# Attention over sources: five groups in different stages per round, and TensorE's order written anew

## What is computed

```python
feat   = concatenate([x[src], edge_weights, x[dst]], axis=1)     # 64 + 16 + 64
h      = relu(feat @ W_att1.T + b_att1)                          # 144 wide
scores = (h @ W_att2.T + b_att2)[:, 0]
m      = segment_max(scores, src)
e      = exp(scores - m[src])
denom  = segment_sum(e, src)
msg    = segment_sum(e / denom[src] * lin_x[dst], src)
```

## Time and profile before

| | us |
|---|---|
| median of 3 runs | 23699.2 (23693.9 to 23703.35) |
| the profiled execution | 23729.27 |
| its span | 23727.5 |
| `source_attention` in it: first gather to last sum | 14451.5 to 19048.4 |
| POOL's 3520 gathers in it (L1724) | 3350.7 busy |
| TensorE's granted clock over the span | 0.625 of full |

### The profile page before, as it was taken

How to read it: one execution, slowest core, us unless ns; L and a number is a source line. 1 busy time by engine, 2 the same in 40 slices (tenths; PEclk the granted TensorE clock), 3 DMA queues, 4 the chain that set the end, 5 groups by cost and what they waited for, 6 DMA issues and landing times. The chain is left out here.

```text
span 23727.5 us, 309845 instructions
## 1 busy us (share of the span) xinstructions
PE 8267.3 (35%) x52022; PEld 6762.3 (29%) x52023; DVE 10675.2 (45%) x28947; ACT 6494.6 (27%) x15429; POOL 16160.3 (68%) x16650
## 2 busy tenths in 40 slices
PE   2431111111111111111111116888888753333334
PEld 1110000000000111111111115777787733333333
DVE  4744444444444322222222216777777554444445
ACT  0012222222222133333333323555555411111111
POOL 1057777777777477777777774777777527777773
PEclk7755555555555555555555557999999755555555
DMA  9223333333333122222222225777777823333333
GB/s 413 82 61 78 81 80 79 79 81 79 78 81 80 43 73 72 71 72 72 71 72 72 71 58 61 86 86 86 86 86 86 66 37 60 60 60 60 60 60 34
DMA packets 2547246, 1881.33 MB, mean 79 GB/s; under 512 B 1939077, under 2 KB 2190275, under 8 KB 2525087
## 3 DMA queue, kind: packets, MB, share of 16 engines
q1 hardware_dynamic: 1766148, 1106.93, 21.6%
q0 software_dynamic: 536736, 602.92, 15.8%
q10 hardware_dynamic: 244252, 170.38, 2.5%
HBM read 1244.80 MB, written 635.40 MB: 79 GB/s over the span
## 5 line engine op out<-in xcount | busy, mean ns | idle before, releaser
L1724 POOL DMA_INDIRECT H<-tab,a_rs x3520 | 3350.7, 952 | 1434.6 <-issue 970.7
L1994 POOL DMA_INDIRECT g_G<-tab,g_rs x3232 | 3065.4, 948 | 1364.6 <-issue 1000.9
L912 POOL DMA_INDIRECT PT<-tab,m_idx x3125 | 3209.2, 1027 | 955.1 <-issue 952.4
L891 POOL DMA_INDIRECT rec<-PT,posi x3125 | 3064.9, 981 | 952.9 <-issue 952.6
L912 POOL DMA_INDIRECT PT<-tab,t_idx x3125 | 2976.5, 952 | 957.8 <-issue 952.1
L1107 PE MATMUL t_ps_z<-t_w,t_eaT 128*128 128x512 f32 x1000 | 671.2, 826 | 5563.9 <-DVE ACC L1081 2789.4
L2075 PE MATMUL g_ps_a<-g_zr,g_oh 128*128 128x64 f32 x6464 | 1586.5, 427 | 2578.9 <-ACT g_zr L2056 2144.2
L2075 PEld LDWEIGHTS g_ps_a<-g_zr,g_oh 128*128 128x128 f32 x6464 | 1438.7, 327 | 2726.7 <-issue 1996.5
L1107 PEld LDWEIGHTS t_ps_z<-t_w,t_eaT 128*128 128x128 f32 x1000 | 265.7, 291 | 5987.9 <-issue 5984.8
L1042 DVE TENSOR_TENSOR t_ps_z<-t_ps_z,PT 128x1600 f32<-128x1600 f32 x125 | 229.1, 1833 | 3256.9 <-DMA PT<-tab,t_idx 3256.9
L2024 DVE TENSOR_TENSOR ACC<-ACC,g_ps_a 128x64 f32 x3232 | 715.5, 221 | 1925.7 <-DVE ACC L2024 1550.0
(11 more groups left out here) (423 smaller groups left out, 23574.2 us busy)
## 6 DMA issues: line engine op xcount, KB each, us to landing
PT<-expand SPq DMA_DIRECT2D x250, 800.0 KB, 4.5
rec<-H SPq DMA_DIRECT2D x88, 1640.0 KB
a_rs<-rec SPq DMA_DIRECT2D x880, 164.0 KB
a_row<-keyc SPq DMA_DIRECT2D x880, 128.0 KB
sums<-t_So SPq DMA_DIRECT2D x125, 850.0 KB
expand<-H ACTq DMA_DIRECT2D x80, 1250.0 KB
PT<-in_ea SPq DMA_DIRECT2D x625, 160.0 KB
maxima<-m_So SPq DMA_DIRECT2D x125, 800.0 KB
```

The lines of the kernel that those rows point to most:

```text
L891: pool.indirect_dma_start(rec, bass.IndirectOffsetOnAxis(ap=self.posi[:, q, t:t + 1], axis=0), rbi[:, q, t, :], None).then_inc(self.s_sc[q ...
L912: pool.indirect_dma_start(G[:, q, c, :], None, table, bass.IndirectOffsetOnAxis(ap=idx[:, q, c:c + 1], axis=0)).then_inc(s_g[q], 16)
L1724: pool.indirect_dma_start(G[:, k, t, 0:D], None, tab3, bass.IndirectOffsetOnAxis(ap=rs[:, k, t, 1:2], axis=0)).then_inc(s_g[k], 16)
L1994: pool.indirect_dma_start(G[:, k, t, :], None, tab3, bass.IndirectOffsetOnAxis(ap=rs[:, k, t, 1:2], axis=0)).then_inc(s_g[k], 16)
```

## The change

Every stage of a group moves to its own round, so that DVE and PE each work on five groups in one round:
- DVE: scores(g), maxima(g-1), exponents(g-2), keep(g-4), onehots(g+2), weighted(g-2).
- PE: node_sums(g-3), feature_rows(g+1), key_rows(g+1), turn(g+2), spread(g), edge_maxima(g-1).
- ACT: high_part(g), rescale(g-1), weights(g-2), penalty(g), turned(g+2), local_keys(g+5), features(g+5).

`ps_z`, `ss`, `hi`, `mn`, `dd` and `p` get two slots and `lg` four; `ps_a` has one slot where it had two. The table `M` goes: the old maximum is the last group's maximum times `same` plus `less`, two tables made once from `blk` (1 and 0 where the next group is of the same block, else 0 and -LOW), so ACT reads no block number; DVE reads one in `keep`, right ahead of its use, in every round. PE gets four more `settle`. SP's and POOL's programs stay, but for a count of 3 in POOL's first wait. POOL's wait for `node_sums` of group g - 8 stays too, and `node_sums` of a group now stands in round g+3 where it stood in g+1, while its `turn` stands in g-2 where it stood in g-3.

```diff
-                G, oh = in_place_of_h(ctx, ("a_G", U, GW), ("a_oh", SLOTS, P))
+                taken = T * (U * GW + SLOTS * P)
+                assert taken + NG <= NB * D
+                G = hw[:, 0:T * U * GW].rearrange("p (k t c) -> p k t c", k=U, t=T)
+                oh = hw[:, T * U * GW:taken].rearrange("p (k t c) -> p k t c", k=SLOTS, t=T)
+                same = hw[:, taken:taken + NG]
+                less = sbl("less", [P, NG])
...
-                ps_z = ps_in(ctx, "a_ps_z", [P, 2, 512])
+                ps_z = ps_in(ctx, "a_ps_z", [P, 2, 2, 512])
                 ps_lb = ps_in(ctx, "a_ps_lb", [P, GE])
                 ps_m = ps_in(ctx, "a_ps_m", [P, 512])
-                ps_a = ps_in(ctx, "a_ps_a", [P, 2, 512])
-                zv = [ps_z[:, b, 0:tpb * width].rearrange("p (t c) -> p t c", t=tpb) for b in range(2)]
+                ps_a = ps_in(ctx, "a_ps_a", [P, 512])
...
+                        dve.memset(same[:, 0:1], 0.0).then_inc(s_set, 1)
+                        dve.tensor_tensor(same[:, 1:NG], blk[:, 1:NG], blk[:, 0:NG - 1], ALU.is_equal).then_inc(s_same, 1)
+                        dve.wait_ge(s_set, 3)
+                        dve.wait_ge(s_same, 1)
+                        dve.tensor_scalar(less[:], same, LOW, -LOW, ALU.mult, ALU.add).then_inc(s_same, 1)
...
-                        def maxima(g, k, r, b):
+                        def maxima(g, k, r):
+                            q = k % 2
                             dve.wait_ge(s_lb, g + 1)
                             dve.wait_ge(s_pen, g + 1)
                             dve.wait_ge(s_mo, g + 1)
-                            at_least(dve, s_mb, g)
-                            at_least(dve, s_me, g)
+                            at_least(dve, s_me, g - 1)
+                            at_least(dve, s_corr, g - 1)
+                            at_least(dve, s_mn, g)
                             settle(dve)
-                            dve.tensor_tensor_reduce(junk[:], ps_lb[:], pen[:, k % 2], 1.0, mo[:, k % 2:k % 2 + 1], ALU.add, ALU.max, mn[:]).then_inc(s_mn, 1)
+                            dve.tensor_tensor_reduce(junk[:], ps_lb[:], pen[:, q], 1.0, mo[:, q:q + 1], ALU.add, ALU.max, mn[:, q:q + 1]).then_inc(s_mn, 1)
...
-                        def keep(g, k, r, b):
+                            dve.tensor_scalar(dd[:, q], dd[:, q], 70.0, None, ALU.min).then_inc(s_d, 1)
+
+                        def keep(g, k, r):
+                            b = dve.value_load(blk[0:1, bass.ds(g, 1)], min_val=0, max_val=NB)
                             acc = ACC[:, bass.ds(b, 1), 0:VC].rearrange("p a c -> p (a c)")
                             dve.wait_ge(s_corr, g + 1)
                             dve.wait_ge(s_acc, g + 1)
                             at_least(dve, s_done, g)
                             settle(dve)
-                            dve.scalar_tensor_tensor(acc, acc, corr[:, k % SLOTS:k % SLOTS + 1], ps_a[:, k % 2, 0:VC], ALU.mult, ALU.add).then_inc(s_done, 1)
-
-                        blocks = [None] * U
-
-                        def body(g, k, r):
-                            at = (g, k, r)
+                            dve.scalar_tensor_tensor(acc, acc, corr[:, k % SLOTS:k % SLOTS + 1], ps_a[:, 0:VC], ALU.mult, ALU.add).then_inc(s_done, 1)
+
+                        def body(*at):
                             stage(scores, 0, NG, *at, unroll=U)
-                            stage(weighted, 1, NG, *at, unroll=U)
+                            stage(maxima, 1, NG, *at, unroll=U)
+                            stage(exponents, 2, NG, *at, unroll=U)
+                            stage(keep, 4, NG, *at, unroll=U)
                             stage(onehots, -2, NG, *at, unroll=U)
-                            older = None
-                            if not isinstance(g, int) or g >= 2:
-                                older = blocks[k - 2] if k >= 2 else block_of(g - 2)
-                            if not isinstance(g, int) or g < NG:
-                                blocks[k] = block_of(g)
-                                maxima(g, k, r, blocks[k])
-                            if older is not None:
-                                keep(g - 2, (k - 2) % U, r + (k - 2) // U, older)
-                            stage(exponents, 0, NG, *at, unroll=U)
+                            stage(weighted, 2, NG, *at, unroll=U)
                         onehots(0, 0, 0)
                         onehots(1, 1, 0)
-                        pipeline(dve, NG, body, 2, unroll=U)
+                        pipeline(dve, NG, body, 4, unroll=U)
...
                         def node_sums(g, k, r):
                             pe.wait_ge(s_oh, g + 1)
-                            at_least(pe, s_done, g - 1)
+                            at_least(pe, s_done, g)
+                            settle(pe)
                             for t in range(T):
-                                mm = pe.matmul(ps_a[:, k % 2, 0:VC], oh[:, k % SLOTS, t, :], G[:, k, t, 0:VC],
+                                mm = pe.matmul(ps_a[:, 0:VC], oh[:, k % SLOTS, t, :], G[:, k, t, 0:VC],
                                                start=(t == 0), stop=(t == T - 1))
                             mm.then_inc(s_acc, 1)
 
                         def body(*at):
+                            stage(node_sums, 3, NG, *at, unroll=U)
                             stage(feature_rows, -1, NG, *at, unroll=U)
+                            stage(key_rows, -1, NG, *at, unroll=U)
+                            stage(turn, -2, NG, *at, unroll=U)
                             stage(spread, 0, NG, *at, unroll=U)
-                            stage(key_rows, -1, NG, *at, unroll=U)
-                            stage(edge_maxima, 0, NG, *at, unroll=U)
-                            stage(node_sums, 1, NG, *at, unroll=U)
-                            stage(turn, -3, NG, *at, unroll=U)
+                            stage(edge_maxima, 1, NG, *at, unroll=U)
                         turn(0, 0, 0)
+                        turn(1, 1, 0)
                         feature_rows(0, 0, 0)
                         key_rows(0, 0, 0)
-                        turn(1, 1, 0)
-                        turn(2, 2, 0)
-                        pipeline(pe, NG, body, 1, unroll=U)
+                        pipeline(pe, NG, body, 3, unroll=U)
...
-                            act.activation(corr[:, k % SLOTS:k % SLOTS + 1], mn[:], ACT.Exp, bias=mo[:, k % 2:k % 2 + 1], scale=-1.0).then_inc(s_corr, 1)
-                            act.copy(M[:, bass.ds(block_of(g), 1)], mn[:]).then_inc(s_mb, 1)
+                            act.activation(corr[:, k % SLOTS:k % SLOTS + 1], mn[:, q:q + 1], ACT.Exp, bias=mo[:, q:q + 1], scale=-1.0).then_inc(s_corr, 1)
                             if not is_group(g, NG - 1):
-                                act.wait_ge(s_mb, g + 1)
-                                old_maximum(*after(g, k, r, U))
-
-                        def block_of(g):
-                            return act.value_load(blk[0:1, bass.ds(g, 1)], min_val=0, max_val=NB)
-
-                        def old_maximum(g, k, r):
-                            at_least(act, s_corr, g - 1)
-                            act.copy(mo[:, k % 2:k % 2 + 1], M[:, bass.ds(block_of(g), 1)]).then_inc(s_mo, 1)
...
                             stage(high_part, 0, NG, *at, unroll=U)
+                            stage(rescale, 1, NG, *at, unroll=U)
+                            stage(weights, 2, NG, *at, unroll=U)
+                            stage(penalty, 0, NG, *at, unroll=U)
                             stage(turned, -2, NG, *at, unroll=U)
                             stage(local_keys, -5, NG, *at, unroll=U)
                             stage(features, -5, NG, *at, unroll=U)
-                            stage(penalty, -1, NG, *at, unroll=U)
-                            stage(rescale, 0, NG, *at, unroll=U)
-                            stage(weights, 0, NG, *at, unroll=U)
-                        act.wait_ge(s_set, 2)
-                        old_maximum(0, 0, 0)
+                        act.wait_ge(s_set, 3)
+                        act.wait_ge(s_same, 2)
+                        act.copy(mo[:, 0:1], mo[:, 0:1]).then_inc(s_mo, 1)
                         for g in range(5):
                             local_keys(g, g, 0)
-                            if g < 4:
-                                features(g, g, 0)
+                            features(g, g, 0)
                         for g in range(2):
                             turned(g, g, 0)
-                        penalty(0, 0, 0)
-                        features(4, 4, 0)
-                        pipeline(act, NG, body, 0, unroll=U)
+                        pipeline(act, NG, body, 2, unroll=U)
```

(28 more changed lines are left out.)

50 lines of the change are left out of this document (26 added, 24 removed).

## The result

The changed kernel takes 27020.6 us, median of 4 runs (26994.0 to 27026.5), against 23701.3 for the kernel before on the same chip: ratio 1.1399, 95% interval 1.1379 to 1.1418. Forecast were 26100 us and a range up to 26900. It is slower through the ring of waits that was forecast; the size lies 120 us outside the range.

What follows compares the result with a forecast made beforehand. POOL's gathers bound the kernel at 5.03 us a group; a new ring of 7.9 us gives 825 x (7.9 - 5.03) = 2368, + 28 (last groups) + 5 (drain) = 2401 us, so 26100 us, range 24850 to 26900.

Steps and rivals of the forecast that it cites:

- the ring of waits that was forecast: From one spread over maxima, exponents, keep, node_sums, feature_rows, key_rows and turn to the next spread, closed by ps_a's single slot.
- The bound: Main part before the change: POOL's gathers set the pace, 5.03 us a group, for 825 groups.
- No slower: Rival: keep(g-4) comes early, PE's sums never wait and POOL stays the bound: 23700; chance 0.04.
- faster: Rival: as no slower, and the last groups gain too, at most 29 us; chance 0.01.
- The length of the ring: The hops of one round on PE and DVE sum to 6.45 us at full clock, 9.83 at half.
- maxima wait for the spread in nearly every round: Sign expected in the new profile: DVE's maxima(g-1) held by PE's spread(g-1), a link of the ring.
- The clock: PE's granted clock taken as 0.73 from the last groups' stretch, 54% of the time at the lower level.
- The prediction's 7.9 us: Length of a main-part round, mixing 9.83 us at the lower clock level (0.54) and 6.45 at full (0.46).
- the last 55: Padding groups, 7.6 us each by transfers, 7.9 by the loop; 0.5 us added each, 28 us.
- Low in most rounds: Rival: PE's clock is low in most rounds, 9.83 us a round, 27790 in all; chance 0.1.
- the sum's own 24905: Rival that the clock holds: 6.45 us a round, 24905, or 24450 at 5.92; chance 0.2.
- The zeros for ACT, SP, the `settle`s and the tables: These other edits were priced at nothing; the settles at 165 us at most.

Runs made afterwards that it cites:

- fill40: The changed kernel with 40 products that nobody reads put into PE's rest after edge_maxima, each round: 24782.9 us, ratio 1.0458.
- keep_first: The changed kernel with one line of DVE's round moved, keep(g-4) first, ahead of scores(g): 23698.2 us, ratio 1.0002.
- fill20: The changed kernel with 20 unread products per round in PE's rest after edge_maxima: 25165.9 us, ratio 1.0618.
- number_early: The changed kernel with keep's block number read ahead of maxima, not right ahead of keep: 25897.7 us, ratio 1.0928.
- number_fill28_beside: The changed kernel with the block number read ahead of maxima and 28 unread products in PE's rest: 24537.9 us, ratio 1.0353.
- before_one_slot: The kernel before with a single buffer for the node sums (ps_a), its order kept: 29062.4 against 29035.3 us, ratio 1.0004.

## Why the prediction was wrong in size

**The bound and the ring: right.** 825 groups at POOL's 5.03 us became rounds of one ring, and two moves of one line each undo it. "No slower" and "faster" fall.

**The length of the ring: right within 2% at both levels of the clock.** Mean distances of the starts, from all rounds of the change (15000 to 21500), beside fill40 (15000 to 18000) at full clock, in us; the third column is the 99th percentile of each distance in the change, taken for its length at half clock (whole rounds of the change take 7.83 to 9.69 us):

| from, to | change | fill40 | half |
|---|---|---|---|
| node_sums, feature_rows | 1.43 | 0.91 | 1.74 |
| feature_rows, key_rows | 1.94 | 1.04 | 2.02 |
| key_rows, first scores | 1.95 | 1.22 | 1.97 |
| first scores, maxima | 1.38 | 0.92 | 1.73 |
| maxima, exponents | 0.67 | 0.67 | 0.68 |
| exponents, keep | 1.20 | 1.20 | 1.22 |
| keep, node_sums | 0.39 | 0.39 | 0.43 |
| sum | 8.96 | 6.35 | 9.79 |

Predicted were 6.45 and 9.83. Single hops were off by up to 0.16 us and cancelled: keep after the second exponents instruction 1.01 for 0.89, node_sums 0.91 for 1.02. One place in the ring was named wrongly. The prediction let it run key_rows, turn, spread, maxima and gave the scores slack; at full clock the way is key_rows, scores, maxima (2.13 us, where the predicted hops give 1.04 + 0.47 + 0.78 = 2.29). In fill40 the maxima never wait for the spread; in the change they do in 452 of 725 rounds. So "maxima wait for the spread in nearly every round" was half wrong.

**The clock: the step that failed.** The change's surplus over fill40, 2.61 us a round, lies in the four rows with PE's products; the three behind them don't move. Of the 9.79 - 6.35 = 3.44 us that the low level can cost, 76% is paid. The prediction's 7.9 us pays (7.9 - 6.45) / (9.83 - 6.45) = 43%. The difference, 1.06 us a round over 825 groups, is 875 us of the 921 missed; the last 55 took 8.84 us each where 8.1 were forecast, 41 us more. The failed step reads "The stretch nearest to the new loop is that of the last groups ... I take 0.73". It failed twice. The clock of the change was 0.64. And a mean clock over time isn't the share of the products that ran low: 0.64 is 72% of the time low, which by the prediction's own formula gives 8.6 us, not 8.96, since much of the full level was granted while PE rested. The two rows of the round shown above have 1.00 for the rest and 0.54 for the products; from 15000 to 21500 the clock's own records put 71% of PE's resting time and 13% of its busy time at the full level. The last groups' 0.73 was a mean over rounds of 4.3 to 16.1 us, with rests for transfers; it was no model of a rest of 2.45 us in each round. fill40 shows the term by itself: PE's rest filled, the clock is 1.00 and the round 6.34 us.

The rivals weren't weighed well either. "Low in most rounds" got 0.1, and the truth lies 55% of the way from the forecast to it (8.96 between 7.9 and 9.83). The Trainium skill, TensorE: Matmul & The Clock Gate, section HAM oscillation, describes a loop whose every tile starts cold after a wait for a transfer. The trace agrees in part. The rest here comes from another engine's work, and no round ran at full clock throughout (the shortest took 7.83 us, against 6.35). But the products right behind the rest weren't the coldest: by the table node_sums paid 63% of what the low level can cost it, feature_rows 92% and key_rows 97%.

**Small terms and signs.** PE's rest was 2.45 us (forecast 2.2) and the clock 0.64, just under the 0.65 to 0.85 named. The node sums' wait is there (2104.6 us idle), but the profile puts most of it down to "issue" and 91 of 725 to keep; that it is keep's wait is told by their distance, 0.38 to 0.43 us in every round. The range's lower end, 24850, is 55 us under the sum's own 24905, and nothing hangs on it. Turn hardly waited for gathers any more (2 times), the gap ahead of keep was 0.85 (forecast 0.7), and POOL started 446 gathers per 1000 us (some 500). The zeros for ACT, SP, the `settle`s and the tables hold as far as the runs show: keep_first has them all at 23698, where POOL would hide small ones, and the ring at full clock is no longer than its hops without them.

## What to carry to other kernels

Before moving stages, write down the ring of waits that closes within one round, through every single-buffered tile; if it is longer than the bound, one stage in the wrong place costs everything (here 3319 us, and one line brings it back). Price such a ring at both clock levels, and don't take a mean clock from a stretch whose rests differ: here a rest of 2.45 us in every round cost 76% of the difference between the levels, and one of 1.47 us (fill20) 14%. The instruction that a profile names ahead of an idle gap need not be its cause: here 0.73 us of a gap put down to ACT was a register read, which moved within the ring still cost 0.4 us at full clock.

## What the runs showed that was not expected

- More work made the kernel faster: 40 unread products a round took the granted clock from 0.64 to 1.00 and 8.3% off the time; 20 took it to 0.92. Reading a register ahead of its use shortened PE's rest, and the clock was 0.70. The five kernels of the ring by PE's rest (idle time ahead of the node sums' weight loads, per round, 15000 to 18000, the change 15000 to 21500):

| kernel | rest, us | granted clock | round, us |
|---|---|---|---|
| the change | 2.45 | 0.64 | 8.96 |
| number_early | 1.82 | 0.70 | 7.71 |
| fill20 | 1.47 | 0.92 | 6.83 |
| number_fill28_beside | 0.76 | 1.00 | 6.05 |
| fill40 | 0.39 | 1.00 | 6.34 |

- The same kernel before took 23.7 ms on some chips and 28.8 to 29.0 ms on two others. On one of these the groups of before_one_slot take 7.79 us (15922.2 to 22774.1), DVE pauses with its inputs ready, and the compute instructions have their usual lengths. Two rows of DVE, here `keep` (L1788) and `exponents` (L1777) of the kernel before:

```profile
16505.30 0.28 DVE L1788 SCALAR_TENSOR_TENSOR ACC<-ACC,a_corr,a_ps_a 128x65 f32 x1
16509.04 0.16 DVE L1777 TENSOR_TENSOR a_dd<-a_lg,a_ps_m 128x4 f32<-128x4 f32 x1 [3.46 <-DMA PT<-expand]
```

The last input of the second, edge_maxima's product, had started at 16505.57 and took 0.27 us. The transfer that the profile names belongs to another layer. With one gather of four a group takes 4.46 us at a clock of 1.00. What holds the engines stays open.
